# An integration loop with its stages in two PSUM banks by turns, its seeds merged and issued ahead, and its last sum and clip in one operation

## What is computed

```python
def _derivative(q, p, drive, coupling, bias):
    dq = q - q ** 3 / 3.0 - p + drive + jnp.tanh(q) @ coupling.T + bias
    dp = EPSILON * (q + ALPHA - BETA * p)
def _rk4_step(...):            # four derivatives, each from the one before
    q_next = clip(q + DT / 6.0 * (dq1 + 2 * dq2 + 2 * dq3 + dq4), -20, 20)
    p_next = clip(p + DT / 6.0 * (dp1 + 2 * dp2 + 2 * dp3 + dp4), -20, 20)
```

## Time and profile before

| | us |
|---|---|
| median of 3 runs | 602.54 (602.47 to 604.92) |
| the profiled execution, its own time | 602.0 |
| its span in the trace | 600.1 |
| integration loop in the trace (first seed to the last clip) | 294.05 to 587.26 |

### The profile page before, as it was taken

One profiled execution on the slowest core, in us unless ns is written; L12 is line 12 of the kernel. 1 busy time (PEld: TensorE's weight loads), 2 busy tenths in 40 slices (PEclk: granted clock), 3 DMA queues, 4 the chain that ended last, 5 costly groups with the idle time before them and its releaser, 6 DMA issues.

```text
span 600.1 us, 17261 instructions
## 1 busy us (share of the span) xinstructions
PE 571.6 (95%) x6460; PEld 519.0 (86%) x6460; DVE 499.8 (83%) x1523; ACT 390.9 (65%) x959; POOL 250.8 (42%) x399
## 2 busy tenths in 40 slices
PE   9999999999999988999978999999999999999997
PEld 8999999999999887888867888888788887888885
DVE  3777777676777767758789999999999999999996
ACT  3545454454544454455557888888888898888785
POOL 0423323233232244320254556556556555555550
PEclk9999999999999999989999999999999999999999
DMA  8500000000000001410000000000000000000001
GB/s 265 182 2 2 1 1 2 1 1 2 2 1 1 19 3 32 127 42 4 2 1 1 11 20 19 11 19 19 10 19 19 11 20 10 19 19 11 19 19 37
DMA packets 13170, 15.08 MB, mean 25 GB/s; under 512 B 1760, under 2 KB 11296, under 8 KB 13088
## 3 DMA queue, kind: packets, MB, share of 16 engines
q1 hardware_dynamic: 13088, 13.98, 7.2%
HBM read 9.78 MB, written 4.19 MB: 23 GB/s over the span
## 4 chain that ended last, share of the span: by engine, by line
PE 78%; ACT 11%; DVE 8%; issue 3%; POOL 0%; DVEq 0%; ACTq 0%; POOLq 0%
PE PS L475 23%; PE PS L322 18%; PE PS L345 13%; ACT q_s L788 5%; PE PS L406 4%; PE PS L453 4%; PE PS L527 4%; PE PS L548 4%; PE PS L511 2%; ACT k_s L769 2%; PE PS L426 2%; PE PS L385 2%; PE PS L328 2%; DVE PS L1081 1%; ACT PS L772 1%
## 5 line engine op out<-in xcount | busy, mean ns | idle before, releaser
L475 PE MATMUL PS<-k_s,h_s 128*128 128x128 f32 x1024 | 160.7, 285 | 4.7 <-DVE PS L1055 2.5
L475 PEld LDWEIGHTS PS<-k_s,h_s 128*128 128x128 f32 x1024 | 131.7, 191 | 21.9 <-DVE PS L1069 9.8
L322 PE MATMUL PS<-part 128*128 128x256 f32 x900 | 115.6, 286 | 0.0
L322 PEld LDWEIGHTS PS<-part 128*128 128x128 f32 x900 | 109.8, 191 | 0.0
L769 ACT ACTIVATE k_s<-h_s 128x128 f32<-128x128 f32 x256 | 69.0, 306 | 50.4 <-DVE h_s L1170 29.0
L345 PE MATMUL PS<-big,wrk 128*128 128x128 f32 x744 | 88.4, 275 | 1.7 <-DVE big L926 1.7
L345 PEld LDWEIGHTS PS<-big,wrk 128*128 128x128 f32 x744 | 85.8, 192 | 2.3 <-DVE big L926 2.3
L1238 POOL COPY h_s<-big 128x256 f32<-128x256 f32 x32 | 21.5, 671 | 129.2 <-DVE big L926 129.2
L475 PE MATMUL PS<-h_s 128*128 128x128 f32 x384 | 74.2, 275 | 0.0
L475 PEld LDWEIGHTS PS<-h_s 128*128 128x128 f32 x384 | 58.3, 192 | 0.0
L664 ACT ACTIVATE big<-big 128x256 f32<-128x256 f32 x32 | 13.3, 417 | 63.2 <-DVE big L908 63.2
(11 more groups left out here) (188 smaller groups left out, 1226.8 us busy)
## 6 DMA issues: line engine op xcount, KB each, us to landing
out<-q_s SPq DMA_DIRECT2D x32, 128.0 KB, 1.7
x_s<-in_xT SPq DMA_DIRECT2D x14, 256.0 KB, 6.0
k_s<-in_wgT SPq DMA_DIRECT2D x4, 208.0 KB, 3.1
k_s<-in_wuT SPq DMA_DIRECT2D x4, 208.0 KB, 2.6
k_s<-in_wih SPq DMA_DIRECT2D x3, 256.0 KB, 4.1
wrk<-in_whh SPq DMA_DIRECT2D x3, 256.0 KB, 4.9
h_s<-in_wdT SPq DMA_DIRECT2D x3, 256.0 KB, 3.8
x_s<-in_xT SPq DMA_DIRECT2D x4, 128.0 KB, 3.7
```

Source lines behind the costliest of these rows:

```text
L322: r = pe.matmul(p, y, x, start=i == 0, stop=i == len(passes) - 1)
L475: return pe.matmul(PS[:, m, 0:128], w, x, start=False, stop=True, skip_group_check=True)
```

## The change

It keeps every product and every sum of the integration, and changes where they lie and when they are issued.

- **Two banks by turns.** A stage's two halves lie side by side in one bank, `stage_bank(slot)`, bank 0 for stages 1 and 3 and bank 1 for stages 2 and 4. Each seed is one operation of 128x256.
- **Seeds ahead.** `seed_1` of the next step comes right behind the last sum of this one, `seed_2` behind it at the head of the step, `seed_3` ahead of `t2`, `seed_4` ahead of stage 3's `cubic`.
- **Identity products ahead.** `linear` adds the identity products of stage s+1 behind the coupling products of stage s, so that `coupled` has four products in every stage, ordered by the half of tanh that they need. Both halves end with one semaphore.
- **Last sum and clip in one.** q and p are kept multiplied by `lam`, so that the last sum needs no factor, and one custom VectorE operation (add, then min, then max) of 128x128 for each half takes the place of the `nexts` and the clip.
- **GpSimd's sums.** `u3` and `W3` come first and wait for `seed_2`, then `t1`; `uz`, `WZ` and `dq` wait for `t2`; the output sum waits for `seed_4`; the next step's `v1` follows the new p.
- `t4` comes ahead of stage 4's `cubic`, and the factors that `lam` brings are put into constants.

```diff
+        stage_bank = lambda slot: PS[:, slot % 2, 0:256]
...
+            def linear(slot, scale, x):
+                pe.wait_ge(s_seed, slot + 1)
+                if slot % 4 > 1:
+                    pe.wait_ge(s_next, q_next(slot // 4, slot % 4 - 2, 1))
                 for m in range(2):
-                    pe.wait_ge(s_seed, 2 * slot + m + 1)
-                    pe.wait_ge(s_th, 2 * slot + 1)
-                    add(m, coupU[:, 0, m * 128:(m + 1) * 128], cm(th[slot % 2], 0))
-                    pe.wait_ge(s_th, 2 * slot + 2)
-                    r = add(m, coupU[:, 1, m * 128:(m + 1) * 128], cm(th[slot % 2], 1))
-                    if x is not None:
-                        r = add(m, scale, cm(x, m))
-                    r.then_inc(s_ps, 1)
+                    add(slot, m, scale, cm(x, m))
+            def coupled(slot):
+                pe.wait_ge(s_seed, slot + 1)
+                for k in range(2):
+                    pe.wait_ge(s_th, 2 * slot + k + 1)
+                    for m in range(2):
+                        r = add(slot, m, coupU[:, k, m * 128:(m + 1) * 128], cm(th[slot % 2], k))
+                r.then_inc(s_ps, 1)
...
                 coupled(4 * t)
+                linear(4 * t + 1, id_q1, qn[t % 2])
...
-                coupled(4 * t + 1, id_q1, qn[t % 2])
+                coupled(4 * t + 1)
+                linear(4 * t + 2, id_s2, qs[0])
...
-                coupled(4 * t + 2, id_s2, qs[0])
+                coupled(4 * t + 2)
+                linear(4 * t + 3, id_z3, qs[1])
...
-                for m in range(2):
-                    if t:
-                        ve.wait_ge(s_next, 8 * t - 1 + m)
-                    ve.tensor_tensor(PS[:, m, 0:128], I_at(t)[:, m], cm(pn[t % 2], m), ALU.subtract).then_inc(s_seed, 1)
+                ve.scalar_tensor_tensor(two(stage_bank(0)), two(pn[t % 2]), -1 / lam, I_at(t), ALU.mult,
                                         ALU.add).then_inc(s_seed, 1)
...
+            def last_next(t):
+                ve.wait_ge(s_w, 4 * t + 4)
+                ve.wait_ge(s_ps, 4 * t + 4)
+                for m in range(2):
+                    ve._custom_dve(bass.dve_ops.TENSOR_ADD_SAT, out=cm(qn[(t + 1) % 2], m), in0=cm(stage_bank(3), m),
+                                   in1=cm(w_, m), s0=CLAMP * lam, s1=-CLAMP * lam).then_inc(s_q, 1)
...
-                seed_1(t)
+                seed_2(t)
...
-                seed_2(t, 0)
-                if t < T - 1:
-                    ve.wait_ge(s_t1, t + 1)
-                    ve.wait_ge(s_next, 8 * t + 2)
-                    ve.scalar_tensor_tensor(t2, t1, horner[1], qs[0], ALU.mult, ALU.add).then_inc(s_t2, 1)
...
-                seed_2(t, 1)
+                seed_3(t)
                 if t >= 1:
                     ve.wait_ge(s_tq, t)
                     ve.reciprocal(q_at(t - 1, 4), q_at(t - 1, 1)).then_inc(s_s1, 1)
+                if t < T - 1:
+                    ve.wait_ge(s_t1, t + 1)
+                    ve.scalar_tensor_tensor(t2, t1, horner[1], qs[0], ALU.mult, ALU.add).then_inc(s_t2, 1)
...
+                seed_4(t)
                 cubic(4 * t + 2, qs[1])
...
-                nexts(4 * t + 3, lambda m: PS[:, m, 128:256])
-                for m in range(2):
-                    ve.wait_ge(s_next, 8 * t + 7 + m)
-                    ve.tensor_scalar(cm(qn[(t + 1) % 2], m), PS[:, m, 128:256], CLAMP, -CLAMP, ALU.min,
-                                     ALU.max).then_inc(s_q, 1)
+                cubic(4 * t + 3, qs[2])
+                last_next(t)
+                if t < T - 1:
+                    seed_1(t + 1)
...
+                po_.wait_ge(s_seed, 4 * t + 2)
+                po_.wait_ge(s_dr, drive_done(t))
+                po_.tensor_scalar(u3, p, -n2 / lam, 0.0, ALU.mult, ALU.add).then_inc(s_u3, 1)
+                po_.wait_ge(s_u3, t + 1)
+                po_.tensor_tensor(two(W3), two(u3), I_at(t), ALU.add).then_inc(s_W3, 1)
                 if t < T - 1:
                     if t:
                         po_.wait_ge(s_q, 2 * t)
                     po_.wait_ge(s_v1, t + 1)
                     po_.tensor_tensor(t1, v1, q, ALU.add).then_inc(s_t1, 1)
                     po_.wait_ge(s_t2, t + 1)
+                po_.tensor_scalar(uz, p, -n3 / lam, 0.0, ALU.mult, ALU.add).then_inc(s_uz, 1)
+                po_.wait_ge(s_uz, t + 1)
+                po_.tensor_tensor(two(WZ), two(uz), I_at(t), ALU.add).then_inc(s_WZ, 1)
+                po_.wait_ge(s_next, q_next(t, 0, 1))
+                po_.tensor_tensor(dq, qs[0], q, ALU.subtract).then_inc(s_dq, 1)
```

More of the change, by code:

```diff
@@ L58, in build @@
     own = (3 + 3 / c, 3.0, 3.0, 3 + 3 / c)
-    of_ps = (c4, c4, 2 * c4, c4 / 3)
+    lam = 3 / c4
+    of_ps = (3.0, 3.0, -6.0)
+    q_next = lambda t, s, m: 6 * t + 2 * s + m + 1
     with ExitStack() as ctx:
@@ L1047, in seed_1, with seed_2, seed_3 @@
                 ve.wait_ge(s_dr, drive_done(t))
-                for m in range(2):
-                    if t:
-                        ve.wait_ge(s_next, 8 * t - 1 + m)
-                    ve.tensor_tensor(PS[:, m, 0:128], I_at(t)[:, m], cm(pn[t % 2], m), ALU.subtract).then_inc(s_seed, 1)
-            def seed_2(t, m):
-                ve.wait_ge(s_next, 8 * t + 1 + m)
-                ve.scalar_tensor_tensor(PS[:, m, 0:128], cm(pn[t % 2], m), -(1 - A), I_at(t)[:, m], ALU.mult,
-                                        ALU.add).then_inc(s_seed, 1)
-            def seed_3(t, m):
+                ve.scalar_tensor_tensor(two(stage_bank(0)), two(pn[t % 2]), -1 / lam, I_at(t), ALU.mult,
+                                        ALU.add).then_inc(s_seed, 1)
+            def seed_2(t):
+                if t:
+                    ve.wait_ge(s_q, 2 * t)
+                ve.scalar_tensor_tensor(two(stage_bank(1)), two(pn[t % 2]), -(1 - A) / lam, I_at(t), ALU.mult,
+                                        ALU.add).then_inc(s_seed, 1)
+            def seed_3(t):
                 ve.wait_ge(s_W3, t + 1)
-                ve.wait_ge(s_next, 8 * t + 3 + m)
-                ve.scalar_tensor_tensor(PS[:, m, 0:128], cm(qn[t % 2], m), (1 + 2 * A * kap) / (2 * c4), cm(W3, m),
-                                        ALU.mult, ALU.add).then_inc(s_seed, 1)
+                ve.wait_ge(s_next, q_next(t, 0, 1))
+                ve.scalar_tensor_tensor(stage_bank(2), qn[t % 2], (1 + 2 * A * kap) / 6, W3, ALU.mult,
+                                        ALU.add).then_inc(s_seed, 1)
             def seed_4(t):
@@ L1088, in vector @@
             weight_quant(0)
+            seed_1(0)
             for t in range(T):
@@ L1111, in vector @@
                     ve.tensor_reduce(q_at(i, 0), pq, X, ALU.max, apply_absolute_value=True).then_inc(s_red, 1)
[L1112 to L1119 removed]
+                nexts(4 * t, qs[0])
                 if t >= 1:
@@ L1134, in vector @@
                     product(t - 2, 1)
-                nexts(4 * t + 1, lambda m: cm(qs[1], m))
-                seed_3(t, 0)
-                seed_3(t, 1)
+                nexts(4 * t + 1, qs[1])
                 if t < 2:
@@ L1145, in vector @@
                     ve.tensor_reduce(h_at(i, 0), hN[i % 2], X, ALU.max, apply_absolute_value=True).then_inc(s_mxh, 1)
+                seed_4(t)
                 cubic(4 * t + 2, qs[1])
-                nexts(4 * t + 2, lambda m: cm(qs[2], m))
-                seed_4(t)
+                nexts(4 * t + 2, qs[2])
                 if t >= 2:
@@ L1156, in vector @@
                     ve.wait_ge(s_t2, t + 1)
-                    ve.wait_ge(s_next, 8 * t + 4)
                     ve.scalar_tensor_tensor(t3, t2, horner[2], qs[1], ALU.mult, ALU.add).then_inc(s_t3, 1)
-                cubic(4 * t + 3, qs[2])
-                if t < T - 1:
-                    ve.wait_ge(s_t3, t + 1)
-                    ve.wait_ge(s_next, 8 * t + 6)
-                    ve.scalar_tensor_tensor(t4, t3, horner[3], qs[2], ALU.mult, ALU.add).then_inc(s_t4, 1)
                 if t >= 2:
@@ L1166, in vector @@
                     ve.reciprocal(h_at(i, 4), h_at(i, 1)).then_inc(s_s2, 1)
-                nexts(4 * t + 3, lambda m: PS[:, m, 128:256])
-                for m in range(2):
-                    ve.wait_ge(s_next, 8 * t + 7 + m)
-                    ve.tensor_scalar(cm(qn[(t + 1) % 2], m), PS[:, m, 128:256], CLAMP, -CLAMP, ALU.min,
-                                     ALU.max).then_inc(s_q, 1)
+                if t < T - 1:
+                    ve.wait_ge(s_t3, t + 1)
+                    ve.wait_ge(s_next, q_next(t, 2, 1))
+                    ve.scalar_tensor_tensor(t4, t3, horner[3], qs[2], ALU.mult, ALU.subtract).then_inc(s_t4, 1)
+                cubic(4 * t + 3, qs[2])
+                last_next(t)
+                if t < T - 1:
+                    seed_1(t + 1)
             def middle_scale(i):
```

74 lines of the change are left out of this document (30 added, 44 removed).

## The result

| | before | after |
|---|---|---|
| median | 602.54 us (5 runs, 601.89 to 604.92) | 599.46 us (5 runs, 598.6 to 600.0) |
| ratio | | 0.9941, 95% interval 0.9919 to 0.9964 |
| profiled execution, own time and span | 602.0, 600.1 | 599.46, 597.7 |

Faster by 0.6%. The forecast was 590 us with a range of 582 to 598: the sign is right, the size is a quarter of what was forecast, and the range is missed by 1.5 us. A second set of runs of the changed kernel on another chip gave 0.9943.

What follows compares the result with a forecast made beforehand. The bound was taken as a ring of waits between two nearly full queues, TensorE and VectorE. 11.0 us from 29 steps plus 1.2 from steps 0 to 2 gave 602.0 - 12.2 = 589.8, median 590 us, range 582 to 598.

Steps and rivals of the forecast that it cites:

- 9.09 - 8.71 = 0.38 us in each of 29 steps: Loop steps after the first three: each falls from 9.09 to 8.71 us, 11.0 us in all.
- The last sum's start: End of a step: VectorE's last sum starts 0.03 us after the last product's record ends, at 8.23.
- `linear` behind its wait: TensorE, stage 4's identity products: they wait for `seed_4` until 5.94, then take 0.45 us.
- the 0.2 to 0.3 that I named: TensorE idle some 0.2 to 0.3 us a step until `seed_4`, because the long reduce stands ahead of that seed.
- my 6.16 less 0.45: TensorE: gate product at 6.16 by its work alone, 0.45 being the two identity products ahead of it.
- The hold: VectorE's `seed_3` overlaps GpSimd's `t1`; both read SBUF and exclude each other, so it goes 0.21 us late, at 2.54.
- My rival without it (583.5 us): `seed_3` runs undisturbed at 2.33, giving 8.50 us a step and 583.5 us; chance 15%.
- same 0.4 us each: Steps 0 to 2, though disturbed, each gain 0.4 us, 1.2 us together; estimated between 0 and 0.8 each.
- After the loop: Work behind the last step: nothing changes there.
- the hidden tile's rounding: It held TensorE idle 0.35 us a step; now done by 1.8, with two identity products filling that gap.
- the third rival: Custom operation dear or small waits adding up in the ring: 8.8 to 9.0 us a step, 593 to 600; chance 20%.
- the two it named: Custom operation at 0.24 to 0.36 us for each half, or GpSimd's `dq` late for `seed_4`.

Runs made afterwards that it cites:

- e1: Changed kernel with the custom last operation replaced by a built-in one of the same shape, so the new q is not the true sum: 596.26 us, ratio 0.992.
- e6: Changed kernel with the cubic term and the products counting into one semaphore, so each sum waits once instead of twice: 593.98 us, ratio 0.9889.
- e3: Changed kernel with stage 4's identity products behind the gate product on TensorE instead of ahead of it: 593.15 us, ratio 0.9871.
- e2: Changed kernel with GpSimd's `t1` cut to 16 of its 256 columns from step 1 on: 590.64 us, ratio 0.9827.
- e8: Changed kernel with GpSimd's `t1` computed a second time into a tile nobody reads or waits for: one single run, 611.67 us beside 603.32 for before.
- v4: Changed kernel relaid on VectorE, GpSimd and TensorE, with one wait ahead of each sum and the output sum not held until `seed_4`: 587.53 us, ratio 0.9743.
- e4: Changed kernel with `product`'s second half moved ahead of the scale operation and `seed_3`: 601.36 us, ratio 1.0004.
- v2: Changed kernel with `product`'s second half, `uz` and stage 3's `cubic` moved earlier, stage 4's identity products behind the gate product: 591.4 us, ratio 0.9837.

## Why the prediction was wrong in size

The step that failed is the term "9.09 - 8.71 = 0.38 us in each of 29 steps". The direction and the mechanisms in it stand, and it is mis-sized: a step takes 8.95, so the term is 0.15 us. With zero at the end of the second half of the new q (440.89 + 0.49 = 441.38), the schedule and the trace read:

| event | forecast | after |
|---|---|---|
| `seed_1`, `seed_2` | -0.08, 0.25 | -0.08, 0.25 |
| `nexts` of stage 1 | 1.81 | 1.81 |
| `seed_3` | 2.54 | 2.60 |
| long reduce | 4.56 | 4.62 |
| `seed_4` | 5.49 | 5.55 |
| `linear` of stage 4 | 5.94 | 6.02 |
| gate product | 6.39 | 6.57 |
| stage 4's coupling | 7.14 | 7.27 |
| end of its last record | 8.20 | 8.32 |
| last sum | 8.23 | 8.47 |
| its end, one step | 8.71 | 8.96 |

1. **The last sum's start: 0.03 forecast, 0.15 measured, half of the error.** I took 0.03 from before, where the last `nexts` follows the end of the products by that the earlier trace rows. But that row is half 1. In the code of before the wait for the cubic term stands ahead of the loop over the halves and the wait for the products inside it, so half 1 had one wait ahead of it and half 0 two. In the new kernel both halves wait for one count, and it is the first operation, with two waits, that the products release. The row was of another form than the operation it was to price. e1 rules out the custom operation but for 0.03, and e6 shows that with one wait the gap is 0.04, custom operation and all, and the step 0.10 shorter.
2. **`linear` behind its wait: 0.45 forecast, 0.55 measured.** The records are 0.71 long after a wait and 0.61 in e3 without one. The wait itself is 0.06, not the 0.2 to 0.3 that I named, because TensorE reaches that place later than I laid out: at about 5.96 (447.40 less 441.38 and the 0.06), where my 6.16 less 0.45 gave 5.71. What the pair costs the step is 0.10 by e3. Against this the gate was 0.05 quicker than its term (0.70).
3. **The hold was right, and reached further.** `seed_3` was forecast 0.21 late and was 0.27 late. L1137, a scale operation on 128x3 that I had left out of the reckoning, was issued while `t1` ran and was held itself, and `seed_3` came behind it. In e2, without the hold, `seed_3` stands at 2.40 and not at my 2.33, so the hold is 0.20 of the 0.27. The other 0.07 is there without it; whether it comes from the scale operation or from the two waits ahead of `seed_3` was not tested. e2 and e8 show the hold from both sides. The Trainium skill (SBUF — State Buffer, Who interferes with whom) says that a VectorE instruction with two SBUF inputs and a GpSimd instruction that reads SBUF exclude each other whole, and the trace agrees down to the smallest operations: 0.47 instead of 0.15 us. My rival without it (583.5 us) is out.
4. **The first three steps: -1.2 forecast, +0.2 measured.** VectorE's and GpSimd's timelines of after in step 0:

```profile
297.69 0.94 DVE L1073 SCALAR_TENSOR_TENSOR PS<-h_s 128x256 f32<-128x256 f32 x1
...
301.60 0.43 DVE L1080 SCALAR_TENSOR_TENSOR PS<-q_s 128x256 f32<-128x256 f32 x1 [0.62 <-POOL q_s L1307]
```
```profile
296.17 0.67 POOL L1293 TENSOR_SCALAR h_s<-h_s 128x256 f32<-128x256 f32 x1 [9.35 <-DVE PS L1067]
297.62 0.73 POOL L1300 TENSOR_TENSOR q_s<-h_s 128x256 f32<-128x256 f32 x1
...
300.50 1.07 POOL L1307 TENSOR_TENSOR q_s<-h_s 128x256 f32<-128x256 f32 x1
```

   `seed_3` is held for 0.5 us by `t1`, and `seed_4` waits 0.62 for `dq` (L1307), both of which my flat "same 0.4 us each" had passed over. v4, which has `uz` ahead of the wait for `t2`, has `dq` in time and takes 302.44 - 293.78 = 8.66 in step 0, against 9.14. It also has `cubic` ahead of `seed_4` and one wait instead of two, so how much of the 0.48 is `dq`'s isn't shown. Step 1 of after repeats both losses: `seed_3` takes 0.89 us (307.32) and `seed_4` waits 0.62 (311.30). In step 2 VectorE waits 1.18 us for the up product ahead of its first `product` (316.57), where it waited 0.80 before (314.55). So the three steps gained nothing together, by delays that the traces show and no run took apart.
5. **After the loop: 0 forecast, +0.5 measured.** No run was made for it. The traces place 0.28 of it: VectorE's first `reduce` behind the loop waits for the transpose of q, and that stands behind the up product in TensorE's queue. Before, the up product (L574) starts at 586.59, 0.19 ahead of the clip, and the `reduce` (L1189) at 587.71, 0.93 behind it. After, the up product (L585) starts at 583.95, 0.07 behind the start of the last sum, right behind ScalarE's silu (L838, 582.94 + 0.95 = 583.89), and the `reduce` (L1200) at 585.09, 1.21 behind it. So the clip that fell away bought nothing there. The rest stays open.
6. **Right:** the custom operation at 0.20 us for each half, the fusion at 0.37 a step (0.40 forecast), the merged seeds at 0.33 (0.42 us records), `seed_1` at once behind the last sum with the new p in time, ScalarE and the hidden tile's rounding out of the way, and TensorE's work unchanged.

So a step is off by 0.12 + 0.10 + 0.08 (`linear` of stage 4 later, mostly by the 0.07 in front of `seed_3`) - 0.06 (gate and coupling) = 0.24 us. In the sum of the profiled execution, 12.2 us were forecast and 2.5 came: 6.6 of the missing 9.7 are in steps 3 to 31 (11.0 less 4.4), 1.4 in the first three, 0.5 at the end, and 1.3 in the clock ahead of the loop, 9.8 in all. The case that came is the third rival, small waits that add up in the ring (8.8 to 9.0 us a step, 593 to 600 us), though by other waits than the two it named. It had 20%, and I let the range end at 598, inside its own bounds. That was a second mistake, and that the time fell into this rival's range, by waits that it didn't name, is in part luck.

Of what the changed kernel left behind, the runs found 0.33 us a step (8.95 to 8.62 in v4): alone, the hold gave 0.18, the second wait 0.10 and the gate 0.10, so they overlap a little. e4 shows that they can't be taken one at a time in any order.

## What to carry to other kernels

In a ring of two nearly full queues a sum of saved work says little: write down the schedule of every queue, put each wait's release beside it, and price the operation behind a wait that is released last by a row of the same form: the same engine, the same number of waits ahead of it. Here the difference was 0.1 us in each of two places. An operation that two engines' products release is best given one semaphore that both count into. Sums on GpSimd that read SBUF must be laid clear of every VectorE operation with two SBUF inputs, the tiny ones included (and, by a row below, of rounding operations like the ones in steps 0 to 2), and a move that does so has to be checked for what it delays behind it.

## What the hardware showed that I had not expected

- A VectorE operation with two waits ahead of it starts 0.15 us after the products' end when the second is released last (after), and 0.04 after it with one wait (e6).
- A VectorE operation on 128x3 took 0.47 us (after) instead of 0.15 (e2), and one on 128x2 took 0.49 (v2) instead of 0.14 (v4), beside a GpSimd sum whose result it neither uses nor waits for.
- A weight rounding on VectorE, which has only one SBUF input (L994, 128x832 to bf16), took 1.14 us in step 0 of before (296.56), beside a GpSimd sum that ran from 296.53 to 297.26, and 0.59 alone (294.46). So the hold isn't confined to operations with two SBUF inputs.
- Identity products straight behind a wait take 0.10 us more for four records (0.71 in after, 0.61 in e3) at a granted clock of 1.00. In e4, where the wait was 0.19 us instead of 0.06, they took 0.71 too.
- The stretch ahead of the loop, with identical code, ended anywhere from 291.4 to 295.3 us with a mean granted clock from 1.00 down to 0.96 between 200 and 290 us, which is more than what the change gained.
